# Values of self attention projected at a slot's beginning in the banks of q and k, and a unit's division moved to the middle of the next slot

## The reference, cut to what matters

```python
q = jnp.einsum('bse,hed->bhsd', x, Wq) + bq[None, :, None, :]
k = jnp.einsum('bse,hed->bhsd', x, Wk) + bk[None, :, None, :]
v = jnp.einsum('bse,hed->bhsd', x, Wv) + bv[None, :, None, :]
scores = jnp.einsum('bhsd,bhtd->bhst', q, k) / jnp.sqrt(jnp.float32(DH))
scores = jnp.where(causal[None, None, :, :], scores, -jnp.inf)
attn = jax.nn.softmax(scores, axis=-1)
out = jnp.einsum('bhst,bhtd->bhsd', attn, v)
```

## Time and profile before

| What | Value |
|---|---|
| Median of 3 runs | 430.06 us (429.84 to 430.45) |
| The profiled execution | 428.27 us |
| Its span, first to last instruction | 426.5 us |
| TensorE matmul / weight load | 385.7 / 274.1 us busy |
| VectorE, ScalarE, GpSimd | 307.5, 237.6, 239.8 us busy |

### The profile page before, as it was taken

The page is one execution under the profiler, slowest core; times in us unless marked ns, Lnnn a source line. Parts: engine busy times, 40 slices in busy tenths (PEclk is TensorE's granted clock), DMA queues, the critical chain, the costliest instruction groups (busy, mean ns, idle before and its releaser), DMA issues.

```text
span 426.5 us, 9900 instructions
## 1 busy us (share of the span) xinstructions
PE 385.7 (90%) x3698; PEld 274.1 (64%) x3698; DVE 307.5 (72%) x924; ACT 237.6 (56%) x352; POOL 239.8 (56%) x338
## 2 busy tenths in 40 slices
PE   3779999999999999999999999799999999998821
PEld 1567666776767776677766767577787776544410
DVE  0646887877887777887788877976535655689897
ACT  2335665556665566665666556464512155788941
POOL 3466876556665565655667556465824430231775
PEclk9989999999999999999999999999999999999985
DMA  8012011000000300000000000000000000000001
GB/s 259 12 6 54 3 15 27 4 8 5 5 1 5 100 2 2 3 4 1 2 3 2 2 2 3 0 2 2 3 1 2 2 0 2 2 2 2 25 26 51
DMA packets 41568, 6.96 MB, mean 16 GB/s; under 512 B 38320, under 2 KB 40240, under 8 KB 41392
## 3 DMA queue, kind: packets, MB, share of 16 engines
q1 hardware_dynamic: 41520, 6.32, 9.3%
HBM read 5.12 MB, written 1.05 MB: 14 GB/s over the span
## 4 chain that ended last, share of the span: by engine, by line
PE 64%; DVE 14%; ACT 7%; DMA 7%; issue 4%; SPq 3%; POOLq 0%; POOL 0%; DVEq 0%; ACTq 0%
PE banks L172 11%; PE banks L146 10%; PE banks L214 8%; PE banks L699 7%; DMA shift<-neg_max 6%; PE banks L152 4%; PE banks L191 4%; DVE unused L352 3%; PE banks L130 3%; PE banks L743 3%; PE banks L165 3%; SPq L523 3%; PE banks L756 3%; ACT q_hi L305 2%; PE banks L163 2%
## 5 line engine op out<-in xcount | busy, mean ns | idle before, releaser
L286 ACT ACTIVATE probs<-banks 128x768 f32<-128x768 f32 (+1 forms) x96 | 84.9, 884 | 114.1 <-PE banks L152 114.1
L352 DVE CUSTOM_DVE_ANT_0 unused<-banks,neg_mask 128x512 bf16<-128x512 f32 (+3 forms) x256 | 112.6, 487 | 38.8 <-PE banks L130 38.8
L451 POOL TENSOR_SCALAR_AFFINE_SELECT probs<-probs 128x256 f32<-128x256 f32 x128 | 51.2, 412 | 112.7 <-ACT probs L286 111.3
L172 PE MATMUL banks<-probs,v_nat 128*64 128x256 f32 (+3 forms) x512 | 74.4, 433 | 0.0
L172 PEld LDWEIGHTS banks<-probs,v_nat 128*64 128x64 f32 x512 | 36.6, 137 | 45.3 <-issue 40.5
L152 PE MATMUL banks<-shift,ones_r 64*128 64x256 f32 (+3 forms) x256 | 42.9, 329 | 6.7 <-DMA shift<-neg_max 6.6
L898 POOL TENSOR_TENSOR rstd<-var_e,halves 128x4 f32<-128x4 f32 (+1 forms) x16 | 14.4, 898 | 60.1 <-DVE var_e L974 59.8
L146 PE MATMUL banks<-q_hi,k_hi 64*128 64x256 f32 (+3 forms) x256 | 43.5, 334 | 1.7 <-ACT probs L286 1.7
L361 DVE SCALAR_TENSOR_TENSOR q_lo<-banks,bias_qk,q_hi 128x512 fp32r<-128x512 f32 x32 | 24.0, 751 | 25.8 <-ACT q_hi L305 25.8
L146 PE MATMUL banks<-q_hi,k_lo 64*128 64x256 f32 (+3 forms) x256 | 41.9, 321 | 0.0
L146 PE MATMUL banks<-q_lo,k_hi 64*128 64x256 f32 (+3 forms) x256 | 41.8, 320 | 0.0
(11 more groups left out here) (125 smaller groups left out, 826.1 us busy)
## 6 DMA issues: line engine op xcount, KB each, us to landing
shift<-neg_max SPq DMA_DIRECT2D x256, 0.5 KB, 2.0
attn_t<-w_qkv SPq DMA_DIRECT2D x1, 1344.0 KB, 7.0
attn_t<-xT SPq DMA_DIRECT2D x4, 256.0 KB, 7.2
x_s<-x_nat SPq DMA_DIRECT2D x1, 1024.0 KB, 5.1
wo_s<-wo SPq DMA_DIRECT2D x1, 512.0 KB, 3.9
out<-y_out SPq DMA_DIRECT2D x2, 256.0 KB, 3.1
out<-y_out SPq DMA_DIRECT2D x4, 128.0 KB, 1.7
neg_mask<-causal SPq DMA_DIRECT2D x1, 256.0 KB, 3.8
```

The costliest lines, as they stand in the source:

```text
L172: last = mm(o_ps[HALF[h], j * T:S], v_nat[:, v // 2 % 2, j, v % 2, HALF[h]], p_of(v, j, h, 0, S - j * T), start=(j == 0), stop=(j == NT - 1))
L286: nc.scalar.activation(probs[:, v % 2, AT[j]:AT[j] + 2 * n].rearrange("p (h s) -> p h s", h=2), st[:, :, 0:n], ACT.Exp, scale=D ** -0.5).t ...
L352: last = V.tensor_tensor_reduce(out=unused[:, h, at:at + n], in0=mx[:, h, at:at + n], in1=neg_mask[:, S - n:S], scale=-1.0, scalar=3.0e38, ...
L451: return nc.gpsimd.affine_select(out=blk, in_=blk, compare_op=ALU.is_ge, fill=0.0, base=0, pattern=pattern + [[1, T]], channel_multiplier=-1)
```

## The change

It changes three things in the slots. Both parts of `values` move to the beginning of the slot of their own unit, and into banks 4 and 5, where q and k are projected too. So values wait for `q_lo` and `k_lo` of the unit after (the last readers of these banks), and the projection waits for ScalarE's copy of the values. The division of a unit moves from the end of VectorE's slot into the middle of the next one, between its maxima 1 and `q_lo`. `weigh` now waits for that division and for the value copy, `sums` for `inverse` alone. ScalarE copies the values at the slot's beginning, ahead of its first exponential. In slot 30, `bias` and `context_keys` come behind the projection's place.

The second stage begins in another state (a division is still open, `sums(30)` comes first), and all its lists are reordered, with the same operations. The scalings of normalisations 1/2 (layer norm 1 of batch element 2) and 3/0 go from GpSimd to VectorE, those of 2/1 and 2/2a from VectorE to GpSimd.

```diff
             def sums(v):
                 pe.wait_ge(added, 4 * v + 4)
-                if has(v + 2):
-                    pe.wait_ge(v_out, v + 3)
-                elif v:
-                    pe.wait_ge(o_out, v)
+                if v:
+                    pe.wait_ge(neg_out, v)
...
             def weigh(v):
                 pe.wait_ge(masked, 3 * v + 3)
+                pe.wait_ge(v_out, v // 2 * 2 + 2)
+                if v:
+                    pe.wait_ge(o_out, v)
...
             def values(v, part):
...
                 if part == 0:
-                    if v >= 3:
-                        pe.wait_ge(o_out, v - 2)
+                    if v < LAST:
+                        pe.wait_ge(ql_out, v + 2)
+                        pe.wait_ge(kl_out, v + 2)
+                    else:
+                        pe.wait_ge(v_out, LAST)
...
-                        last = mm(banks[:, 6 + at, 0:4 * D], x[HALF[h], tile:tile + T],
+                        last = mm(aux[at][:, 0:4 * D], x[HALF[h], tile:tile + T],
...
             def project(v, part):
...
-                    if v:
-                        pe.wait_ge(ql_out, v)
-                        pe.wait_ge(kl_out, v)
+                    if v == 1:
+                        pe.wait_ge(ql_out, 1)
+                        pe.wait_ge(kl_out, 1)
+                    elif v:
+                        pe.wait_ge(v_out, v - 1)
...
             def slot(u):
                 if has(u):
+                    values(u, 0)
+                    values(u, 1)
                     scores(u, 0)
                 if has(u + 1):
                     maxima(u + 1, 0)
                 if has(u + 2):
                     project(u + 2, 0)
                 if u == LAST - 1:
-                    bias()
-                    context_keys()
-                if has(u + 1):
-                    values(u + 1, 0)
+                    values(LAST, 0)
+                    values(LAST, 1)
                 if has(u):
                     scores(u, 1)
                 if u == -2:
                     project(u + 2, 1)
                 if has(u + 1):
                     maxima(u + 1, 1)
-                if has(u + 1):
-                    values(u + 1, 1)
                 if has(u + 2) and u > -2:
                     project(u + 2, 1)
+                if u == LAST - 1:
+                    bias()
+                    context_keys()
                 if has(u):
                     scores(u, 2)
...
             def slot(u):
                 if has(u):
+                    values(u)
                     exponentials(u, 0)
+                if u == LAST - 1:
+                    values(LAST)
+                if has(u):
                     exponentials(u, 1)
-                if has(u + 1):
-                    v = u + 1
-                    act.wait_ge(v_done, 2 * v + 2)
...
                 if has(u + 1):
                     maxima(u + 1, 0)
                     maxima(u + 1, 1)
+                if has(u - 2):
+                    normalise(u - 2)
                 if has(u + 2):
                     low_half(u + 2, 0)
...
                 if has(u - 1):
                     inverse(u - 1)
-                    normalise(u - 1)
...
-        SCALED = {"pool": "11 12 13 20 30 22b 31 23b 32a 32b".split(), "dve": "10 21 22a 23a 33a 33b".split()}
+        SCALED = {"pool": "11 13 20 21 22a 22b 31 23b 32a 32b".split(), "dve": "10 12 30 23a 33a 33b".split()}
...
-            scores(31, 0); y(0, 0); sums(30); y(0, 1); scores(31, 1); y(0, 2); context(); y(0, 3); weigh(30)
+            sums(30); scores(31, 0); y(0, 0); scores(31, 1); y(0, 1); y(1, 0); y(0, 2); y(1, 1); y(0, 3)
...
-            inverse(30); add(1, 0); stats(1, 0); normalise(30); scale(1, 0); m(0, 0); m(0, 1); m(0, 2); q(0)
+            normalise(29); add(1, 0); stats(1, 0); scale(1, 0); inverse(30); normalise(30); add(1, 1); stats(1, 1)
```

More of the change, by code:

```diff
@@ L223, in bias @@
                 pe.wait_ge(later_in, LOADS)
-                pe.wait_ge(ql_out, UNITS)
+                pe.wait_ge(v_out, UNITS)
                 for p in range(PAIRS):
@@ L317, in slot, with values @@
                     reciprocal(u - 1)
+            def values(v):
+                act.wait_ge(v_done, 2 * v + 2)
+                if v >= 4:
+                    act.wait_ge(o_done, v // 2 * 2 - 2)
+                nc.scalar.copy(v_nat[:, v // 2 % 2, v % 2 * 2:v % 2 * 2 + 2, :, :].rearrange("p i a d -> p i (a d)"),
+                               banks[:, 4:6, 0:4 * D]).then_inc(v_out, 1)
             def reciprocal(v):
@@ L784, in f @@
                 four(dst, lambda i: xq_t[:, i * T:(i + 1) * T], fkq[:, :], done, False, h)
-            scores(31, 0); y(0, 0); sums(30); y(0, 1); scores(31, 1); y(0, 2); context(); y(0, 3); weigh(30)
-            scores(31, 2); y(1, 0); t(0); y(1, 1); q(0); y(1, 2); m(0, 0); m(0, 1); sums(31); m(0, 2); m(0, 3)
-            y(1, 3); y(2, 0); m(0, 4); weigh(31); m(0, 5); y(2, 1); m(0, 6); m(0, 7); t(1); y(2, 2); r(0); y(2, 3)
-            q(1); s(0, 0); m(1, 0); y(3, 0); m(1, 1); s(0, 1); m(1, 2); y(3, 1); t(2); m(1, 3); p(0, 0); m(1, 4)
@@ L796, in _ @@
-            z(2, "b"); s(3, 3); f(1); p(3, 0); p(3, 1); o(3, 0); o(3, 1); u(3); x(2, "a"); z(3, "a"); z(3, "b")
-            x(2, "b"); f(2, "a"); f(2, "b"); x(3, "a"); f(3, "a"); x(3, "b"); f(3, "b")
+            sums(30); scores(31, 0); y(0, 0); scores(31, 1); y(0, 1); y(1, 0); y(0, 2); y(1, 1); y(0, 3)
+            scores(31, 2); weigh(30); y(1, 2); t(0); y(1, 3); q(0); context(); sums(31); m(0, 0); weigh(31); m(0, 1)
+            m(0, 2); y(2, 0); t(1); m(0, 3); m(0, 4); m(0, 5); q(1); m(0, 6); y(2, 1); m(1, 0); m(0, 7); m(1, 1)
@@ new lines, in _ @@
+            y(2, 2); r(0); y(2, 3); s(0, 0); m(1, 2); y(3, 0); s(0, 1); m(1, 3); y(3, 1); m(1, 4); s(0, 2); m(1, 5)
+            p(0, 0); t(2); y(3, 2); o(0, 0); s(0, 3); m(1, 6); y(3, 3); m(1, 7); p(0, 1); r(1); q(2); s(1, 0)
+            m(2, 0); o(0, 1); m(2, 1); m(2, 2); m(2, 3); t(3); u(0); s(1, 1); m(2, 4); z(0); s(1, 2); m(2, 5)
+            p(1, 0); m(2, 6); s(1, 3); m(2, 7); o(1, 0); r(2); q(3); s(2, 0); m(3, 0); p(1, 1); m(3, 1); m(3, 2)
+            o(1, 1); s(2, 1); u(1); m(3, 3); z(1); s(2, 2); p(2, 0); s(2, 3); m(3, 4); o(2, 0); x(0); m(3, 5)
@@ L799, in _ @@
+            m(3, 6); m(3, 7); p(2, 1); r(3); f(0); o(2, 1); s(3, 0); x(1); u(2); s(3, 1); f(1); z(2, "a"); z(2, "b")
+            s(3, 2); s(3, 3); p(3, 0); p(3, 1); o(3, 0); x(2, "a"); o(3, 1); f(2, "a"); u(3); z(3, "a"); x(2, "b")
+            z(3, "b"); f(2, "b"); x(3, "a"); f(3, "a"); x(3, "b"); f(3, "b")
         @block.scalar
@@ L1042, in fp8 @@
                 V.tensor_tensor(xq[:, b % 2, c], nan, neg, ALU.subtract).then_inc(quant_out, 1)
-            inverse(30); add(1, 0); stats(1, 0); normalise(30); scale(1, 0); m(0, 0); m(0, 1); m(0, 2); q(0)
-            add(1, 1); stats(1, 1); m(0, 3); inverse(31); normalise(31); m(0, 4); m(0, 5); m(0, 6); m(0, 7)
-            add(1, 2); stats(1, 2); q(1); m(1, 0); m(1, 1); m(1, 2); m(1, 3); m(1, 4); m(1, 5); m(1, 6); m(1, 7)
-            q(2); m(2, 0); add(1, 3); stats(1, 3); m(2, 1); m(2, 2); o(0, 0); m(2, 3); m(2, 4); m(2, 5); o(0, 1)
@@ L1054, in _ @@
-            stats(2, 3, "a"); stats(2, 3, "b"); add(3, 2, "a"); scale(2, 3, "a"); stats(3, 2, "a"); add(3, 2, "b")
-            power_of_two(3, "a"); fp8(3, "a"); power_of_two(3, "b"); stats(3, 2, "b"); fp8(3, "b"); add(3, 3, "a")
-            stats(3, 3, "a"); add(3, 3, "b"); stats(3, 3, "b"); scale(3, 3, "a"); scale(3, 3, "b")
+            normalise(29); add(1, 0); stats(1, 0); scale(1, 0); inverse(30); normalise(30); add(1, 1); stats(1, 1)
+            m(0, 0); inverse(31); m(0, 1); q(0); normalise(31); m(0, 2); m(0, 3); m(0, 4); m(0, 5); q(1); m(0, 6)
@@ new lines, in _ @@
+            m(1, 0); m(0, 7); m(1, 1); add(1, 2); m(1, 2); m(1, 3); stats(1, 2); m(1, 4); scale(1, 2); m(1, 5)
+            o(0, 0); m(1, 6); add(1, 3); m(1, 7); stats(1, 3); q(2); m(2, 0); o(0, 1); m(2, 1); m(2, 2); m(2, 3)
+            m(2, 4); m(2, 5); add(2, 0); m(2, 6); m(2, 7); stats(2, 0); o(1, 0); m(3, 0); m(3, 1); o(1, 1)
+            power_of_two(0); m(3, 2); q(3); m(3, 3); add(2, 1); stats(2, 1); fp8(0); m(3, 4); o(2, 0); m(3, 5)
+            m(3, 6); m(3, 7); power_of_two(1); fp8(1); o(2, 1); add(3, 0); stats(3, 0); add(2, 2, "a")
@@ new lines, in _ @@
+            stats(2, 2, "a"); scale(3, 0); add(2, 2, "b"); add(3, 1); stats(2, 2, "b"); stats(3, 1)
+            power_of_two(2, "a"); fp8(2, "a"); o(3, 0); o(3, 1); power_of_two(2, "b"); add(3, 2, "a"); fp8(2, "b")
+            add(2, 3, "a"); stats(2, 3, "a"); add(2, 3, "b"); add(3, 2, "b"); stats(2, 3, "b"); scale(2, 3, "a")
+            stats(3, 2, "a"); stats(3, 2, "b"); power_of_two(3, "a"); fp8(3, "a"); power_of_two(3, "b"); fp8(3, "b")
+            add(3, 3, "a"); stats(3, 3, "a"); add(3, 3, "b"); stats(3, 3, "b"); scale(3, 3, "a"); scale(3, 3, "b")
```

48 lines of the change are left out of this document (17 added, 31 removed), and 14 rows, old and new, of the table USES.

## The result

The changed kernel takes **451.88 us** (450.36 to 453.17, 4 runs) beside 430.23 (429.84 to 430.45, 4 runs) for the kernel before: a ratio of 1.0503 (95% interval 1.0466 to 1.054), 21.6 us slower. The forecast of 437.0 had the sign and not the size: 451.88 lies beyond its upper end of 441.0. Two executions far slower than all others of their kernel, one of a_full (962 us) and one of the kernel before (554 us), are left out of every ratio.

A forecast was written before the change was run, and what follows sets the result against it. TensorE was taken to bound the slots, VectorE's reductions exactly meeting it between maxima 0 and 1. Terms 5.3 + 1.4 − 0.65 + 0.6 + 0 gave +6.7, rounded to +7 on 430.06: 437.0 us, range 433.5 to 441.0.

The forecast's parts named there:

- The hole: Between maxima 0 and 1, TensorE waits for VectorE's reductions once value part 0 leaves: 0.33 us in 16 slots, 5.3.
- 0.70 us in one piece: Slot's beginning: the value parts moved there take 0.35 and 0.36 us, 0.70 together, with the same 12 matmuls a slot.
- the rivals: Whole kernel: no change 430.1 us (chance 0.04), faster 424 us (0.05), slower by more 444.5 us (0.08).
- the signs: Undisturbed slots of 8.9 to 9.1 us, maxima waiting about 0.3 on `neg_max` in over 15, second stage about 125.
- Scores 2 and the second exponential: Before scores 2, TensorE has 0.35 us less to do against 0.25 of slack; charged only in late-`shift` slots, 0.2 each.
- Late copies: Slots with a late `shift`: the wait swallows the hole, but 0.2 us is added in each, 7 × 0.2 = 1.4.
- single slots: Particular slots: −0.3 at the `attn_t` wait, −0.55 at the delayed reductions, about +0.2 for four more; −0.65 together.
- the rival "faster": Wait ahead of `shift` in scores 1: copies leave 0.35 earlier; with other waits gone −6.0, 424 us; chance 0.05.
- The wait on `attn_t`: The 2.6 us wait at values moves to the maxima, behind VectorE's feed-forward weights: −0.3, none left at values.
- Start: Values of unit 0 wait for `k_lo` of unit 1, ahead of the first scores: +0.6, between −0.3 and +1.5.
- Second stage: New hand-written orders with the same operations, some scalings swapped between GpSimd and VectorE: 0, ±2.5 us.
- `k_lo`: Slot's beginning: values wait for `k_lo`, which ends 0.5 us before TensorE arrives; nothing charged.

The follow-up runs named there:

- a_full: Changed kernel, each values part as one tile over all 128 rows (3 matmuls, one bank): 448.01, 444.2 and 446.19 us, ratio 1.0365; profiled again, 443.96 us.
- b_early: Kernel before, values part 0 moved from behind the projection to ahead of maxima 0 (units 3 to 30): 447.35 us, ratio 1.0406.
- b_late: Kernel before, values part 0 moved from ahead of scores 1 to behind it: 439.44 us, ratio 1.0211.
- b_adj: Kernel before, values part 1 moved up directly behind part 0, nothing else: 443.89 us beside 432.62, ratio 1.0276.
- a_exp: Changed kernel, one more 128x128 ScalarE copy between exponentials 0 and 1 and their signal: 459.06 us, ratio 1.0666.
- a_start: Changed kernel, values of unit 0 alone projected in slot -1, in banks 6 and 7, as before the change: 452.49 us, ratio 1.0522.
- a_div: Changed kernel, division back at the end of VectorE's slot, behind the inverse: 450.8 us, ratio 1.0485.
- a_sums: Changed kernel, `sums` issued between the projection and scores 1: 458.21 us, ratio 1.0601.
- a_weigh: Changed kernel, values part 0 of the next unit issued inside `weigh`, ahead of its third tile: 450.54 us, ratio 1.0424.

## Why the prediction was right in direction and wrong in size

**The hole: right in size, with only part of its cause.** I took 0.33 for moving value part 0 out from between the maxima. The changed kernel pays 1.96 − (2.02 − 0.35) = 0.29 there, and b_early, which makes this hole alone, 0.30. I gave it to VectorE's reductions alone. But 0.20 of it falls ahead of scores 1 or in their restart, where exponential 0 binds as well (b_late shows the same 0.20 with the reductions' stretch left whole), and it comes in all of the 30 slots and not in 16, as late copies no longer swallow it: 30 × 0.29 = 8.7 and not 5.3.

**"0.70 us in one piece": the step that failed.** It added two distances from the earlier trace rows as if they were the parts' own costs. They were the costs with scores and maxima between them. Side by side, part 1 waits until part 0 has left the array, and the two take 1.07 (b_adj). The slot's first stretch is 0.36 over the forecast, 10.8 us in 30 slots. Neither the rivals nor the signs that I named had this wait. The Trainium skill's PSUM — Partial Sum Buffer, in its section on bank collisions, says that different row tiles can't write one bank at the same time and that software has to order them: the two parts are such tiles, the wait is the kernel's way of ordering them (26 waits of 0.29 in the changed kernel), and the change didn't touch its code, only what stood in its shadow.

**Scores 2 and the second exponential: seen, and charged in the wrong place.** I wrote that TensorE has 0.35 less to do against 0.25 of slack, and charged it only to slots with a late `shift`. In the others I let the hole cover it, as if the whole hole lay behind scores 1. As part of it lies ahead of them, the cover is missing in every slot: +0.17, 5.1 us. By the starts, 0.06 of it is the restart of maxima 1 behind their wait and 0.11 that of scores 2. a_exp shows the exponentials binding both stretches in full.

**Late copies: wrong sign.** I charged 7 × 0.2 and −0.65 for single slots. All excess over the undisturbed slot fell from 13.8 to 5.4, −8.4 us: the earlier trace rows had six waits of 3.9 us on `shift`, after there are two of 0.6. Such gains are what the rival "faster" counted on, and those from slot 2 on, 6.9 us, are larger than its 6.0. It looks as if a longer slot with as many copies leaves each more time: the excess in slots 2 to 27 is 7.3 us with slots of 8.65, 6.4 with 8.97 (b_late), 1.6 with 9.26 (b_adj) and none with 9.53 (b_early). No run makes the slot longer and nothing else. The wait on `attn_t` at values is gone as forecast; at the feed-forward weights maxima wait 1.3 for `neg_max`, and that slot falls from 11.64 to 10.67.

**Start and slot 30: too small, and missed.** +4.2 against +0.6 for the start, and a_start, which takes the first value pair away, loses in slots 0 and 1 what it wins ahead of them; +2.8 against nothing for slot 30, 1.0 of it the sums themselves. I put all risk of the new lists behind scores 31, and the first entry of the new list, `sums(30)`, waits ahead of it.

**Second stage, division, `k_lo`, clock: as charged.** 125.8 us against 125.4; as the sums of unit 30 (1.0) have left the stretch, the new order costs 1.4, inside the ±2.5; a_div moves the division without effect, and `q_lo` follows it at 189.82 with no idle time; values start 0.79 behind the end of `k_lo` where I left 0.5; the clock is 1.00 from 65 to 310 us. That single stops cost no clock here was in part luck: in b_adj a stop of 2.61 us at the same wait as in the earlier trace rows is followed by a granted clock of 0.74 from 290 to 295.

Against the span: hole +8.7, pause +10.8, scores 2 +5.1, late waits −8.4, start +4.2, slot 30 +2.8, second stage +0.4 are 23.6, 0.6 over the 23.0 measured, since the three slot terms sum to 0.82 and the slot grew by 0.80.

## What to carry to other kernels

A distance between two starts prices an instruction group in its present company only. Before two groups that order each other are put side by side, look for a wait between them in the code and add its length once; and when work leaves a stretch, list every loop that spans the stretch with its slack, as each of them may close, and the first one closing decides where the time reappears. TensorE's busy share can't show any of this: read the weight load's idle time instead.

## What the runs showed of the hardware that I had not expected

**A change of tile shape on TensorE costs 0.10 us each time, and the restart behind it 0.05 to 0.11 more.** From the last matmul of a group to the next group, with the same shape behind it and with another: projection 0.23 and 0.33 (a_sums, from 64 rows by 128 columns to 128 by 64), sums 0.32 and 0.42 (a_sums), `weigh`'s second tile 0.32 and 0.42 (a_weigh), values 0.12 and 0.21 (a_full2). Behind it, scores 0 take another 0.11 (a_full2) and `weigh` another 0.05 (a_weigh, a_sums). A plain stop has the same restart: in scores 1 the second matmul starts 0.28 behind the first at 186.77, in the kernel before 0.17 (201.94, 202.11). The Trainium skill's TensorEngine Tiling (Array Packing), Key Properties, says that changing the tiling mode drains the engine; these runs agree and put a price on it.

**Two accumulating parts into the same banks, ordered by a semaphore, cost 0.36 us over their own work** when nothing stands between them, and about 0.11 with one group of maxima between (b_late).

**A stop of TensorE of 2 to 3 us was followed by its lower clock in some executions and not in others.** After 2.61 us the granted clock stayed at 1.00 in the kernel before and was 0.74 over the next whole 5 us in b_adj; after 2.10 us it stayed at 1.00 in the changed kernel and was 0.50 from 322 to 328.5 in a_start. There the stretch behind it took 3.1 us more.

**A wait on TensorE can hide in its matmul rows.** The slot grew by 0.8 us of 8.65 while the busy share rose by a point.
